# Causal attention of four heads in rounds, with four value products next to each other on four column tiles

## The reference

```python
qkv = x @ Wqkv.T
q, k, v = jnp.split(qkv, 3, axis=-1)
q, k, v = (heads(q), heads(k), heads(v))
logits = jnp.einsum('bhqd,bhkd->bhqk', q, k) * scale
logits = logits + _fourier_bias(alpha, beta, t)[None]
logits = jnp.where(causal[None, None], logits, -jnp.inf)
attn = jax.nn.softmax(logits, axis=-1)
out = jnp.einsum('bhqk,bhkd->bhqd', attn, v)
```

## Time and profile before

| what | us |
|---|---|
| median of 3 runs | 6354.95 |
| lowest and highest run | 6347.94, 6364.27 |
| span of the profiled execution | 6365.1 |

### The profile page before, as it was taken

One profiled execution on the slowest core, in us unless ns is written; L12 is line 12 of the kernel. 1 busy time (PEld: TensorE's weight loads), 2 busy tenths in 40 slices (PEclk: granted clock), 3 DMA queues, 4 the chain that ended last, 5 costly groups with the idle time before them and its releaser, 6 DMA issues. The chain is left out here.

```text
span 6365.1 us, 149552 instructions
## 1 busy us (share of the span) xinstructions
PE 5238.0 (82%) x55030; PEld 3186.2 (50%) x55030; DVE 4208.1 (66%) x5662; ACT 2952.3 (46%) x4796; POOL 2688.6 (42%) x1428
## 2 busy tenths in 40 slices
PE   4745777638888898589999999999899899999996
PEld 3633445412323222156666666666666666666664
DVE  4354111234343444489999888988898889899995
ACT  0001222213333333256666666666666666666663
POOL 0000000020000000277777777777677676767772
PEclk8756889859898999799999999999999999999997
DMA  0000110031101000111112111211211121111111
GB/s 19 0 8 8 30 30 22 22 55 23 20 10 20 10 11 1 39 48 38 37 34 61 35 36 37 58 36 34 60 35 36 35 57 38 33 38 42 35 36 48
DMA packets 154627, 202.75 MB, mean 32 GB/s; under 512 B 42073, under 2 KB 80867, under 8 KB 152815
## 3 DMA queue, kind: packets, MB, share of 16 engines
q1 hardware_dynamic: 154512, 201.17, 13.5%
HBM read 63.67 MB, written 11.53 MB: 12 GB/s over the span
## 5 line engine op out<-in xcount | busy, mean ns | idle before, releaser
L1772 POOL TENSOR_TENSOR d_rnorm<-d_sq_clip,neg_half 128x32 f32<-128x32 f32 x192 | 1048.5, 5461 | 67.0 <-DVE d_sq_clip L1604 66.4
L1762 POOL TENSOR_TENSOR d_qk_swap<-d_qk_raw,d_rot 128x512 f32<-128x512 f32 x768 | 960.1, 1283 | 16.5 <-ACT d_qk_raw L1447 15.3
L931 DVE TENSOR_REDUCE c_mx<-c_ps 128x1 f32<-128x512 f32 (+3 forms) x768 | 422.5, 557 | 710.7 <-PE c_ps L810 704.6
L1221 PE MATMUL d_pair<-d_wqkv,d_xin 128*128 (+1 forms) x1536 | 752.7, 614 | 91.6 <-DVE d_probs L1625 38.8
L99 POOL TENSOR_TENSOR ln_post_rstd<-ln_post_var,neg_half 128x8 f32<-128x8 f32 x16 | 26.6, 1661 | 1831.7 <-DVE ln_post_var L80 1831.7
L909 ACT ACTIVATE c_pt<-c_ps 128x512 f32<-128x512 f32 (+1 forms) x640 | 353.8, 554 | 712.8 <-PE c_ps L825 711.1
L839 PE MATMUL c_ps<-c_pt,c_vg 128*32 128x512 f32 (+3 forms) x1536 | 627.8, 505 | 4.1 <-DVE c_ots L936 4.1
L1749 POOL TENSOR_TENSOR d_probs<-d_probs,d_prec 128x1024 f32<-128x1024 f32 x192 | 369.0, 1922 | 466.6 <-DVE d_prec L1636 466.6
L1233 PE MATMUL d_pair<-ident,d_qk_part 128*128 128x128 f32 x3072 | 431.5, 280 | 142.2 <-DVE d_qk_part L1615 139.2
L1233 PEld LDWEIGHTS d_pair<-ident,d_qk_part 128*128 128x128 f32 x3072 | 359.8, 143 | 325.1 <-issue 242.1
L1586 DVE TENSOR_TENSOR d_qk_part<-d_qk_raw,d_rot 128x1024 f32<-128x1024 f32 x384 | 471.8, 1229 | 47.6 <-issue 34.2
(11 more groups left out here) (248 smaller groups left out, 9687.5 us busy)
## 6 DMA issues: line engine op xcount, KB each, us to landing
d_band<-d_own_t SPq DMA_DIRECT2D x768, 64.0 KB, 2.0
d_band<-d_prev_t SPq DMA_DIRECT2D x576, 64.0 KB, 2.0
d_v_prev<-d_v SPq DMA_DIRECT2D x192, 128.0 KB, 2.3
b_w<-in_L_ffn_w SPq DMA_DIRECT2D x64, 256.0 KB, 3.5
d_band_prev<-d_prev_t SPq DMA_DIRECT2D x192, 64.0 KB, 2.0
d_wqkv<-in_L_ffn_Wqkv SPq DMA_DIRECT2D x6, 1536.0 KB, 8.8
c_qp<-c_q_scratch SPq DMA_DIRECT2D x96, 64.0 KB
c_kp<-c_k_scratch SPq DMA_DIRECT2D x96, 64.0 KB
```

The lines of the kernel that those rows point to most:

```text
L931: eng.tensor_reduce(mx[:, hh, qt, k0 // 512:k0 // 512 + 1], ps[:, S1B[c % 2], 0:nk], AX.X, ALU.max).then_inc(mx_done, 1)
L1221: eng.matmul(bank(QK_AT[u][c]), xin[p][:, :], wqkv[:, bass.ds(par, 1), c * 512:(c + 1) * 512].rearrange("p l n -> p (l n)"), start=True, s ...
L1762: mm = eng.tensor_tensor(qk_swap[:, which, :, out:out + hd], qk_raw[:, which, :, src:src + hd], rot[:, bass.ds(par, 1), which, 1, bass.ds( ...
L1772: eng.tensor_tensor(rnorm[:, :], sq_clip[:, :], neg_half[:, 0:2 * HEADS], ALU.pow).then_inc(rn_ready, 1)
```

## The change

The 40 chunks of a group become 10 rounds of four: a round is the same chunk of all four heads. TensorE's order in a round is: for each head a second score and a first score; then the value products of the round before, piece by piece through the four heads and so through the four column tiles; then, in the first eight rounds, one more first score. The exponentials go into eight buffers (two sets of four). pv_done counts rounds instead of chunks. The output's first block is turned and divided in round 5, the maxima are negated after round 9's reductions and turned after the last values, and the second block is turned behind that, with a wait for m_ready because both use bank MB. In a group's first round the second score comes ahead of the first score. `first`, `largest`, `read_out`, `divided` and `negated` hold the lines that were in the old loops.

```diff
-        pt = [sb(f"pt{k}", [P, 512]) for k in range(4)]
+        pt = [[sb(f"pt{k}_{hh}", [P, 512]) for hh in range(GROUP)] for k in range(2)]
...
-        S2 = [(blk, hh, c, k == 0) for blk in range(2) for hh in range(GROUP) for k, c in enumerate(chunks(blk))]
-        N1, N2 = GROUP * len(S1), len(S2)
-        HALF = sum(1 for s in S2 if s[0] == 0)
-        LAG = 2
-        assert N1 % 2 == 0 and N2 % 4 == 0
+        ROUNDS = [(blk, segs, k == 0) for blk in range(2) for k, segs in enumerate(chunks(blk))]
+        R = len(ROUNDS)
+        HALF = sum(1 for s in ROUNDS if s[0] == 0)
+        N1, N2 = GROUP * len(S1), GROUP * R
+        S1_ROUNDS = R
+        BEHIND = [1] * (R - 2) + [0, 0]
+        TURN_AT, NEGM_AT = HALF + 2, R
...
+                    def second(r, hh):
+                        blk, segs, _ = ROUNDS[r]
+                        bank = S2B[hh]
+                        if r == 0 and hh == 0:
+                            eng.wait_ge(m_in, (G + 1) * 16)
+                        if r >= 1:
+                            eng.wait_ge(exp_done, G * N2 + (r - 1) * GROUP + hh + 1)
...
+                    def values(r):
+
+                        blk, segs, opens = ROUNDS[r]
+                        eng.wait_ge(exp_done, G * N2 + (r + 1) * GROUP)
+                        if r == 0:
+                            eng.wait_ge(vg_ready, G + 1)
+                        if r == HALF:
+                            eng.wait_ge(o_read, 2 * G + 1)
+                        for k, (kt, q0, nq, col, diag) in enumerate(segs):
+                            for hh in range(GROUP):
+                                mm = eng.matmul(ps[32 * hh:32 * hh + 32, OB, q0:q0 + nq], vg[:, kt, hh, :], pt[r % 2][hh][:, col:col + nq],
                                                 start=(opens and k == 0), stop=True, skip_group_check=True, tile_position=(0, 32 * hh))
...
+                        mm.then_inc(pv_done, 1)
+
+                    def turn_out(blk):
+                        eng.wait_ge(o_read, 2 * G + blk + 1)
+                        if blk == 0:
+                            eng.wait_ge(on_ready, 2 * G)
+                        elif maxima:
+                            eng.wait_ge(m_ready, G + 2)
+                        else:
+                            eng.wait_ge(on_ready, 2 * G + 1)
+                        for t in range(4):
+                            mm = eng.transpose(ps[:, MB, t * P:(t + 1) * P], ots[:, blk, t * P:(t + 1) * P], ident[:, :])
+                        mm.then_inc(o_turned, 1)
+
+                    def turn_maxima():
                         eng.wait_ge(negm_ready, G + 2)
                         if live:
-                            eng.wait_ge(on_ready, 2 * G + 2)
+                            eng.wait_ge(on_ready, 2 * G + 1)
                         eng.transpose(ps[0:GROUP * TB, MB, 0:P], negm[:, :], ident[:, :]).then_inc(m_turned, 1)
 
+                    c = 0
+                    for r in range(R + 1):
+                        for hh in range(GROUP):
+                            if live and r < R:
+                                second(r, hh)
+                            if maxima and r < S1_ROUNDS:
+                                first(c)
+                                c += 1
+                        if live and r >= 1:
+                            values(r - 1)
+                        if live and r == TURN_AT:
+                            turn_out(0)
+                        if maxima and r < S1_ROUNDS:
+                            for _ in range(BEHIND[r]):
+                                first(c)
+                                c += 1
+                        if maxima and r == NEGM_AT:
+                            turn_maxima()
+                    if live:
+                        turn_out(1)
...
-                        eng.wait_ge(pv_done, G * N2)
+                        eng.wait_ge(pv_done, G * R)
...
+                        for r in range(R):
+                            width = sum(s[2] for s in ROUNDS[r][1])
+                            for hh in range(GROUP):
+                                eng.wait_ge(s2_ready, G * N2 + r * GROUP + hh + 1)
+                                if r >= 2 and hh == 0:
+                                    eng.wait_ge(pv_done, G * R + r - 1)
+                                eng.activation(pt[r % 2][hh][:, 0:width], ps[:, S2B[hh], 0:width], ACT.Exp).then_inc(exp_done, 1)
...
+                    c = 0
+                    for r in range(R + 1):
+                        if maxima and r < S1_ROUNDS:
+                            for _ in range(GROUP + BEHIND[r]):
+                                largest(c)
+                                c += 1
+                        if live and r == HALF:
+                            read_out(0)
+                        if live and r == TURN_AT:
+                            divided(0)
+                        if maxima and r == S1_ROUNDS - 1:
+                            negated()
+                    if live:
+                        read_out(1)
+                        divided(1)
```

More of the change, by code:

```diff
@@ L630, in chunks @@
                            [(d + 2, 256, 256, 0, True)]]
[L632 to L636 removed]
+        ROUNDS = [(blk, segs, k == 0) for blk in range(2) for k, segs in enumerate(chunks(blk))]
[5 more added lines that the diff above has]
+        TURN_AT, NEGM_AT = HALF + 2, R
+        assert N1 == S1_ROUNDS * GROUP + sum(BEHIND) and TURN_AT < NEGM_AT
         NG = H // GROUP
@@ L799, in body @@
                         eng.sem_inc(passed, 1)
[L800 to L807, removed]
-                            if diag:
[L809 to L839, removed]
-                                                start=(opens and k == 0), stop=True, skip_group_check=True, tile_position=(0, 32 * hh))
-                            mm.then_inc(pv_done, 1)
@@ L842, in body, with first @@
[L842 to L850, removed]
+                    def first(c):
+                        hh, (qt, k0, nk, diag) = c // len(S1), S1[c % len(S1)]
+                        head = (0 if g is None else ((g + 1) % NG) * GROUP) + hh
+                        bank = S1B[c % 2]
+                        if c >= 2:
+                            eng.wait_ge(mx_done, (G + 1) * N1 + c - 1)
+                        if diag:
+                            eng.matmul(ps[:, bank, nk - P:nk], ident_b[:, :], mask_q[:, :], start=True, stop=False, skip_group_check=True)
+                        eng.matmul(ps[:, bank, 0:nk], qp[0:FEAT, bass.ds(head, 1), qt * P:(qt + 1) * P].rearrange("p a q -> p (a q)"),
+                                   kp[0:FEAT, bass.ds(head, 1), k0:k0 + nk].rearrange("p a q -> p (a q)"),
+                                   start=not diag, stop=True, skip_group_check=True).then_inc(s1_ready, 1)
@@ new lines, in second @@
+                    def second(r, hh):
[6 more added lines that the diff above has]
+                        for k, (kt, q0, nq, col, diag) in enumerate(segs):
+                            if diag:
+                                eng.matmul(ps[:, bank, col:col + P], ident_b[:, :], mask_k[:, :], start=(k == 0), stop=False, skip_group_check=True)
+                            head = bass.ds(g * GROUP + hh, 1)
+                            mm = eng.matmul(ps[:, bank, col:col + nq], kp[:, head, kt * P:(kt + 1) * P].rearrange("p a q -> p (a q)"),
+                                            qp[:, head, blk * 512 + q0:blk * 512 + q0 + nq].rearrange("p a q -> p (a q)"),
+                                            start=not diag, stop=True, skip_group_check=True)
+                        mm.then_inc(s2_ready, 1)
@@ L926, in body @@
                     live = g is not None
[L927 to L936, removed]
@@ L946, in body, with largest, read_out @@
-                    if maxima:
+                    def largest(c):
+                        hh, (qt, k0, nk, diag) = c // len(S1), S1[c % len(S1)]
+                        eng.wait_ge(s1_ready, (G + 1) * N1 + c + 1)
+                        eng.tensor_reduce(mx[:, hh, qt, k0 // 512:k0 // 512 + 1], ps[:, S1B[c % 2], 0:nk], AX.X, ALU.max).then_inc(mx_done, 1)
+                    def read_out(blk):
+                        eng.wait_ge(pv_done, G * R + (HALF, R)[blk])
+                        eng.tensor_copy(ots[:, blk, :], ps[:, OB, :]).then_inc(o_read, 1)
```

25 lines of the change are left out of this document (10 added, 15 removed).

## The result

The changed kernel takes 5871.97 us (median of four runs, 5864.99 to 5881.82) against 6356.65 us for the kernel before beside it: a ratio of 0.9241, 95% interval 0.9225 to 0.9256. The forecast was 5888 us. The profiled execution has a span of 5863.8 us, and its own time, 5865.57, is 1.8 us more.

What follows compares the result with a forecast made beforehand. TensorE was taken to bound a group's loop (59.59 of 59.9 us), a chain of waits its end. Savings of 366, 77 and 24 us, together 467, gave 5898 from the span, 5888 for the median; range 5815 to 6030.

Steps and rivals of the forecast that it cites:

- Values in rounds of four: Value products in a group's loop: four column tiles overlap fully, so 32.0 us a group becomes 8.0.
- Two by two: Rival: strict program order gives value products five slots per round, 20.0 us a group instead of 8.0; 6016 us, chance 0.12.
- The loop: A group's loop: VectorE 31.45 us, plus idle 2.4, hold-up and start 1.45, clock 2; last maximum read at 37.3 us.
- two maxima in hand: During a round's values VectorE has 1.24 us of maxima ready, leaving 0.3 us idle in eight rounds, 2.4 a group.
- the two engines come out equal: In the loop TensorE has 30.9 us and VectorE 31.45, so neither hides the other's waits.
- The clock: Around a group's start TensorE runs 3.6 us at half speed, costing 2 us a group.
- The clock stays low: Rival: TensorE waits for VectorE, so the granted clock stays low; 6262 us throughout, about 6020 half the time; chance 0.08.
- The end: Group's end: negation 0.6 us, then an unchanged 5.0 us chain with two transfers, hiding 4.1 us of output work.
- The very last group: Last group of the attention stage, bound by ScalarE: 30.2 us against 54.18, saving 24.
- The sum: Attention stage: savings of 366 us in twelve groups, 77 in three batch ends and 24 in the very last, together 467.
- the engines take turns: Rival: every wait in TensorE's queue is exposed, a round costs 8.6 us, a group 92; about 6650 us, chance 0.03.
- the tiles don't overlap: Rival: value products on different column tiles do not overlap, TensorE 54.9 us, a group 62; 6192 us, chance 0.05.

Runs made afterwards that it cites:

- one tile: Changed kernel with the value products of all four heads sent to the first column tile; ratio 0.9794 to the kernel before.
- Three banks: Changed kernel with three banks for first scores instead of two, and three for second scores instead of four; ratio 0.9137 to the kernel before.
- kernels without masks: The 64 mask products of a group left out: of the changed kernel, ratio 0.9308; of that with three banks and first scores in eight rounds, 5846.40 us.
- two tiles: Changed kernel with its four heads' value products on two column tiles in turn; one run, 5995.74 us.
- three banks and eight rounds: Changed kernel with three banks each for first and second scores, and first scores six to a round in eight rounds; ratio 0.9095 to the kernel before.
- eight rounds: Changed kernel with the first scores six to a round in eight rounds instead of spread over ten; ratio 0.9206 to the kernel before.

## Why the prediction was right

**Values in rounds of four: right.** 8.0 us forecast, 9.6 busy; 32.0 for one tile, 32.6. Two by two would have been 20: a round's eight instructions take 1.00 us, not five slots (2.2), and that rival is out. The prediction derived it from the rule on program order in the Trainium skill ("TensorE: Matmul & The Clock Gate", Part 3), with the two instructions of a product next to each other in the program. In the trace the first four instructions of a round start within 0.02 us of each other and the other four 0.45 later. So one of the two premises fails here, as with the row of eight tiles before; which one stays open, since the trace lists instructions by their start and not by their place in the program.

**The loop: right in its sum, wrong in two terms that cancelled.** The last maximum was forecast at 37.3 us and read at 37.38 in the group shown (36.8 on the mean of twelve). But the hit is luck in part: VectorE's work is 25.95 us, not 31.45, and 69% of the loop, not 75. The step that failed took 0.62 us for each of 48 maxima, the slot of a full one, while half of them are narrower than 512 columns: one of 128 takes 0.29 us (at 1488.27). In return VectorE is idle for 11.4 us, where idle time, hold-up, start and clock were put at 5.85 (2.4 + 1.0 + 0.45 + 2). The cover of "two maxima in hand" was counted once a round, beside the values: 0.3 in eight rounds, 3.4 a group with the 1.0 for the turn. In the trace, on the mean of the twelve groups, VectorE is idle for 4.5 us before the maxima of the first scores behind the values (0.56 each) and for 6.2 more before the other maxima of the rounds, the start of the group included. Three banks, taking 4.0 us off, show much of these waits to be the hand-over. That "the two engines come out equal" holds in its consequence, neither gives its work back alone, but by the waits and not by equal work.

**The clock: right in kind.** It is low at the start of most groups. Of a loop, 4.0 us are at the lower level on the mean of the twelve (none to 6.1), against 3.6 forecast. Its cost was put at 2 us; the group at full clock is 1.6 us shorter than the mean of the others. "The clock stays low" did not happen, but the kernels without masks show that rival's cost on a small scale.

**The end: right in its length, too dear in its worth.** 0.6 and 5.0 us were forecast, 0.59 (1502.50 to 1503.09) and 5.0 measured. Of the 4.1 us counted as hidden, 1.3 is the chain itself up to m_ready, and copy, turn and division are 2.4; taking them out of hiding costs 2.3.

**The very last group: mis-sized.** 30.2 us forecast, 25.36 measured. The 40 exponentials were put at 0.55 + 0.06 us each, 24.4 in all. 0.55 is right as a mean duration; the gap of 0.06 is not there, since neighbours overlap in the trace (eight of 512 columns start 0.53 to 0.64 us apart and last 0.60; two later ones start 0.50 apart), and ScalarE is busy for 19.15.

**The sum.** Twelve groups 12 x 30.97 = 372 (366 forecast), three last of a batch 3 x (67.75 - 41.77) = 78 (77), the very last 54.18 - 25.36 = 29 (24): 479 against 467. The medians differ by 485 us. The other 6 are less than what the work behind the stage varies by.

The rivals in which the engines take turns or the tiles don't overlap are out as well: a round costs 3.2 to 4.2 us on the mean of the twelve groups (from its first exponential to the next round's), not 8.6, and the values are not at 32.

## What to carry to other kernels

Where small products leave columns of the array idle, put products for different column tiles directly behind each other; here two tiles made the products 1.9 times as fast and four tiles 3.4 times, although each product is a pair of instructions. Once TensorE is no longer full, look at how many results the next engine has in hand while TensorE's queue is busy with something else: a third bank gave 4 us of 42 without removing any work. Cost pieces of several widths by the mean over the widths, not by the slot of the widest one. And before you credit a new order with a gain, compare stretches at the same granted clock.

## What the runs showed of the hardware that was not expected

- Less work on TensorE went with a lower clock. Without masks the time at 0.50 in a loop grew from 4.0 to 8.5 us on the mean, and with three banks and eight rounds groups at 1.00 became groups at 0.87. More of its work beside the transfers went with a higher one: eight rounds have eight of twelve groups at 1.00, ten rounds one at 0.99.
- The stage behind the attention took 3728 to 3796 us in kernels that share its code. The two without masks lie highest (3794.2 and 3795.9). Their scores are not masked and the data behind them differ; whether that, or the place of the code, is the cause was not tried.
